# Two of eight feature-major turns taken from TensorE to VectorE block transposes and DMA through DRAM

## The reference

```
x = x + layernorm(attn(layernorm(x)))
x = x + layernorm(ffn(layernorm(x)))

attn(x): q = silu(x Wq1 Wq2);  v = x Wv
         a = exp(log_sigmoid(sigmoid(x Wk1 Wk2)));  k = 1 - a
         h[t] = a[t] h[t-1] + k[t] v[t]            (a scan over the tokens)
         out = q h;  out = out rsqrt(mean(out^2) + eps) norm_w;  return out Wo
ffn(x):  6 blocks: x = gelu(x W1' + b1) W2' + b2 + x      (256 -> 1024 -> 256)
         between blocks: x = layernorm(x) g + b
```

## Time and profile before

| | |
|---|---|
| median of 3 runs | 632.46 us (632.03 to 632.61) |
| profiled execution | 632.11 us |
| its span in the trace | 630.3 us |
| TensorE busy | 620.9 us, 2913 matmuls |
| VectorE / ScalarE / GpSimd busy | 462.5 / 407.1 / 251.8 us |
| TensorE transposes in `turn` (L490) | 56, 272 ns each |
| DMA | 24.10 MB, mean 38 GB/s |

### The profile page before, as it was taken

How to read it: one execution, slowest core, us unless ns; L and a number is a source line. 1 busy time by engine, 2 the same in 40 slices (tenths; PEclk the granted TensorE clock), 3 DMA queues, 4 the chain that set the end, 5 groups by cost and what they waited for, 6 DMA issues and landing times.

```text
span 630.3 us, 9041 instructions
## 1 busy us (share of the span) xinstructions
PE 620.9 (99%) x2913; PEld 518.0 (82%) x2913; DVE 462.5 (73%) x809; ACT 407.1 (65%) x680; POOL 251.8 (40%) x234
## 2 busy tenths in 40 slices
PE   8999999999999999999999999999999999999996
PEld 6878888887888888888888888888888888888886
DVE  6999766977676877677777768766776767677465
ACT  5989986967755666566565656755665665556454
POOL 5685413339225362324432253623255322304033
PEclk9999999999999999999999999999999999999999
DMA  8210000020111020011200110200112000003522
GB/s 289 69 36 0 2 2 0 4 71 34 37 39 40 4 70 6 12 31 37 72 5 2 40 39 15 60 6 7 36 37 72 5 4 5 6 11 77 113 72 68
DMA packets 51599, 24.10 MB, mean 38 GB/s; under 512 B 43104, under 2 KB 47584, under 8 KB 51552
## 3 DMA queue, kind: packets, MB, share of 16 engines
q1 hardware_dynamic: 51264, 23.26, 14.2%
q10 hardware_dynamic: 288, 0.26, 0.1%
HBM read 19.51 MB, written 4.00 MB: 37 GB/s over the span
## 4 chain that ended last, share of the span: by engine, by line
PE 88%; DVE 4%; issue 1%; ACT 1%; POOL 1%; DVEq 0%; ACTq 0%
PE BK L516 44%; PE BK L833 38%; PE BK L634 2%; PE BK L843 1%; PE BK L490 1%; DVE ST L391 1%; DVE BK L616 1%; POOL RN L713 0%; DVE XL L727 0%; PE BK L647 0%; DVE QB L619 0%; DVE OL L625 0%; DVE R L721 0%; DVE MV L394 0%; DVE QB L578 0%
## 5 line engine op out<-in xcount | busy, mean ns | idle before, releaser
L819 ACT ACTIVATE HH<-BK,B 128x512 fp32r<-128x512 f32 x192 | 132.1, 688 | 179.6 <-PE BK L516 177.5
L825 DVE TENSOR_TENSOR HL<-BK,HH 128x512 fp32r<-128x512 f32 x192 | 130.7, 683 | 98.2 <-ACT BK L822 97.5
L516 PE MATMUL BK<-XH,WL 128*128 128x512 f32 x416 | 162.6, 391 | 0.0
L516 PE MATMUL BK<-XL,WH 128*128 128x512 f32 x416 | 162.1, 390 | 0.0
L516 PE MATMUL BK<-XH,WH 128*128 128x512 f32 x416 | 162.0, 389 | 0.0
L833 PE MATMUL BK<-HH,WL 128*128 128x512 f32 x368 | 143.5, 390 | 0.6 <-DVE HL L825 0.6
L833 PE MATMUL BK<-HL,WH 128*128 128x512 f32 x368 | 143.2, 389 | 0.0
L833 PE MATMUL BK<-HH,WH 128*128 128x512 f32 x368 | 143.2, 389 | 0.0
L822 ACT ACTIVATE BK<-BK,B 128x512 f32<-128x512 f32 x192 | 125.4, 654 | 0.0
L516 PEld LDWEIGHTS BK<-XH,WH 128*128 128x128 f32 x416 | 78.1, 188 | 16.5
L516 PEld LDWEIGHTS BK<-XH,WL 128*128 128x128 f32 x416 | 78.1, 188 | 16.2 <-DVE XL L503 0.2
(11 more groups left out here) (136 smaller groups left out, 783.7 us busy)
## 6 DMA issues: line engine op xcount, KB each, us to landing
STG<-in_w SPq DMA_DIRECT2D x24, 512.0 KB, 3.7
G<-sums SPq DMA_DIRECT2D x160, 8.0 KB, 1.7
out<-R SPq DMA_DIRECT2D x16, 128.0 KB, 1.9
X<-in_x SPq DMA_DIRECT2D x3, 512.0 KB, 7.7
R<-turns SPq DMA_DIRECT2D x3, 512.0 KB, 4.2
sums<-P SPq DMA_DIRECT2D x40, 8.0 KB, 1.4
R<-in_wv SPq DMA_DIRECT2D x1, 512.0 KB, 5.8
STG<-in_wo SPq DMA_DIRECT2D x1, 512.0 KB, 6.2
```

What stands on the lines that cost most here:

```text
L516: r = e.matmul(dst, s, m, start=first and i == 0, stop=last and i == len(todo) - 1)
L819: lambda e, ev=ev, hs=hs, bias=bias: e.activation(HH[:, hs, :], bank_of[ev][:, :], ACT.Gelu, bias=bias),
L825: lambda e, ev=ev, hs=hs: e.tensor_tensor(HL[:, hs, :], bank_of[ev][:, :], HH[:, hs, :].bitcast(f32), ALU.subtract), ("hlo", n, j))
```

## The change

`to_features` is new and replaces `turn` in two places: l1 of tile 3 and l3 of tile 2. For each half k, VectorE transposes 32x32 blocks of the tile in R into a buffer, and four DMAs per half write it to DRAM; when all eight have landed, eight DMAs (four per half) read the feature-major tile back into R. From there ScalarE writes XH and VectorE XL. The keys of the two calls: l1 of tile 3 is normalized with key A - 20 instead of A - 11 and enters `to_features` with A - 16 instead of A - 7.5; l3 of tile 2 keeps Z + 13. The buffers lent are SA and TB, and MB; their first uses in `layer_norm` (n = 0) wait for the writes out. Semaphores that nobody waits on are no longer counted up.

```diff
+        FEATS = nc.dram_tensor("feats", (2, 2, 32, 2048), f32, kind="Internal").ap()
...
+        def to_features(key, name, t, place, tmp, ready, last_use, free):
+            slot_free[name, t] = last_use
+            swapped, moved_out, back = f"sw{place}", f"out{place}", f"back{place}"
+            rows = FEATS[place].rearrange("k j (b c m) -> k j (b c) m", b=4, c=4)
+            for k in range(2):
+                op("vector", key + 0.7 * k, [*ready, *free],
+                   lambda e, k=k: e.transpose(tmp[k].rearrange("p (b c i) -> p b c i", b=4, c=4),
+                                              feat(t, k).rearrange("p c (b j) -> p b c j", b=4)), (swapped, k))
+                for g in range(4):
+                    load(key + 1 + 0.7 * k + 0.1 * g, rows[k, :, :, 32 * g:32 * g + 32],
+                         tmp[k][32 * g:32 * g + 32].rearrange("j (b i) -> j b i", i=32), (moved_out, k, g), [(swapped, k)])
+            for k in range(2):
+                for b in range(4):
+                    load(key + 6 + 0.7 * k + 0.1 * b, feat(t, k)[32 * b:32 * b + 32],
+                         FEATS[place, k][:, 512 * b:512 * b + 512].rearrange("j (c m) -> j c m", c=4), (back, k, b),
+                         [(moved_out, 1, 3)])
+            for k in range(2):
+                op("scalar", key + 11 + 0.8 * k, [(back, 1, 3), ("slot" if k else "give", name, t)],
+                   lambda e, k=k: e.activation(by_chunk(XH[:, slot_of[name, t], k, :]), feat(t, k), ACT.Copy),
+                   ("xhi", name, t, k))
+                op("vector", key + 12 + 0.8 * k, [("xhi", name, t, k)],
+                   lambda e, k=k: e.tensor_tensor(by_chunk(XL[:, slot_of[name, t], k, :]), feat(t, k),
+                                                  by_chunk(XH[:, slot_of[name, t], k, :].bitcast(f32)), ALU.subtract),
+                   ("xlo", name, t, k))
...
-                norm(A - 11, "l1", t, R[:, t], x_of, 0.5, raw_done)
-                turn(A - 7.5, "l1", t, [("l1_nm", t, c) for c in range(4)], ("v", t, 3))
+                norm(A - (20 if t == NT - 1 else 11), "l1", t, R[:, t], x_of, 0.5, raw_done)
+                if t == NT - 1:
+                    to_features(A - 16, "l1", t, 0, [SA[:, :], TB[:, :]], [("l1_nm", t, c) for c in range(4)], ("v", t, 3), [])
+                else:
+                    turn(A - 7.5, "l1", t, [("l1_nm", t, c) for c in range(4)], ("v", t, 3))
...
-            turn(Z + 13, "l3", t, [("l3_nm", t, c) for c in range(4)], ("mm1", t, 7))
+            if t == 2:
+                to_features(Z + 13, "l3", t, 1, [MB[:, k, :] for k in range(2)], [("l3_nm", t, c) for c in range(4)], ("mm1", t, 7), [])
+            else:
+                turn(Z + 13, "l3", t, [("l3_nm", t, c) for c in range(4)], ("mm1", t, 7))
...
-                if done is None:
+                if done is None or done[0] not in waited:
                     continue
...
-                if done is not None:
+                if done is not None and done[0] in sems:
                     last.then_inc(sems[done[0]][0], step)
```

More of the change, by code:

```diff
@@ L657, in sandwich @@
             stats(Z + 1, "l2", t, p_of, lambda c, t=t: [("proj", t, m) for m in range(4)], 0.4)
-            norm(Z + 4.5, "l2", t, R[:, t], p_of, 0.3, [("turn", "l1", t, k) for k in range(2)])
+            norm(Z + 4.5, "l2", t, R[:, t], p_of, 0.3, [("turn", "l1", t, k) for k in range(2)] if t < NT - 1 else [("xlo", "l1", t, k) for k in range(2)])
             for c in range(4):
@@ L679, in before @@
                 return [(x[:-1], n - 1, 1) if x in ("nn1", "ctr1") else (x, n - 1) for x in names if n]
-            op("gpsimd", E + 1.5, [("y", n, 0), ("y", n, 1), *before("tr2")],
+            op("gpsimd", E + 1.5, [("y", n, 0), ("y", n, 1), *before("tr2"), *([("out0", 1, 3)] if n == 0 else [])],
                lambda e: e.tensor_tensor(by_chunk(SA[:, :]), feat(t, 0), feat(t, 1), ALU.add), ("sum1", n))
-            op("vector", E + 3.2, [("sum1", n), *before("red2")], lambda e: e.transpose(TB[:, :], SA[:, :]), ("tr1", n))
+            op("vector", E + 3.2, [("sum1", n), *before("red2"), *([("out0", 1, 3)] if n == 0 else [])], lambda e: e.transpose(TB[:, :], SA[:, :]), ("tr1", n))
             op("vector", E + 3.9, [("tr1", n)],
@@ L690, in layer_norm @@
                ("tot1", n))
-            op("vector", E + 10.2, [("tot1", n), *before("ctr1")],
+            op("vector", E + 10.2, [("tot1", n), *before("ctr1"), *([("out1", 1, 3)] if n == 0 else [])],
                lambda e: e.transpose(MB[:, 0, :].rearrange("p (b f) -> p b f", f=32),
@@ L713, in layer_norm @@
                lambda e: e.tensor_tensor(RN[:, :], VN[:, :], MH[:, :], ALU.pow), ("rsd", n))
-            op("vector", E + 25.5, [("rsd", n), *before("nn1")],
+            op("vector", E + 25.5, [("rsd", n), *before("nn1"), *([("out1", 1, 3)] if n == 0 else [])],
                lambda e: e.transpose(MB[:, 1, :].rearrange("p (b f) -> p b f", f=32),
@@ L922, in sandwich, with resolve @@
         slot_of.update(slots)
+        def resolve(w):
+            return prior[w] if w[0] in ("ring", "slot", "claim", "give") else None if w[0] == "after" else w
+        waited = set()
+        for q in order.values():
+            for o in q:
+                waited.update(w[0] for w in map(resolve, o[2]) if w is not None)
         owner = {}
@@ L936, in sandwich @@
                 place[done] = sems[s][1]
-        def resolve(w):
-            return prior[w] if w[0] in ("ring", "slot", "claim", "give") else None if w[0] == "after" else w
         def issue(eng, name):
```

## The result

The changed kernel is slower: 637.09 us median of 6 runs (635.88 to 639.53), against 632.5 us for the kernel before in the same session (6 runs). The ratio is 1.0082, with an interval of 1.0067 to 1.0097. The forecast was 630.7 us, and 637.09 lies above its range. The profiled execution of the changed kernel took 636.01 us (span 634.2), the one before 632.11 (630.3), so it is 3.9 us that the trace has to show.

A forecast was written before the change was run, and what follows sets the result against it. TensorE was taken to bound the kernel, busy 620.9 of 630.3 us; two removed turns gave -1.8 us and all other terms 0, so 632.46 - 1.8 = 630.7 us, range 628.9 to 634.2 us.

The forecast's parts named there:

- Two turns, -1.8 us: On TensorE, removing two groups of eight transposes, at 84 and 116.86 us, saves 0.89 us each, 1.8 us in all.
- better: Rival, chance 0.15: TensorE's HL and OL waits go too, as the tail leaves 145 to 151 us; 629.9 us.
- Slack of 2.7 us for tile 3's first norm: XL ready at 89.1 us, TensorE first takes XH at 91.81 us, so the DRAM route costs nothing.
- slower, by landing: Rival, chance 0.05: tile 3's first norm's transfers land at 5.4 us each way, TensorE stands 4.1 us; 634.8 us.
- The last norm of tile 2 in SP's order: New transfers delay the first feed-forward norm's `put1` 5.9 us and gathers 7.0 us; tile 2's XL has 12 us slack; no cost.
- The tail of the first feed-forward norm, "I leave it at 0": VectorE's R and XL at 145.6 to 150.3 us move 0 to 7 us; HL wait may go or grow; taken as 0.
- slower, by VectorE: Rival, chance 0.13: tile 2's swaps and blocked subtractions at 116 to 133 us delay OL or HL, +3.5 us; 634.2 us.
- "The order on every engine is planned anew ..., so each case has about 0.6 us to either side": Replanning every engine's order from the changed list was given about 0.6 us of spread around each case.
- Two SBUF operands in the subtractions: VectorE's four XL = R - XH might lose 0 to 4.2 us to GpSimd on the shared port; taken as 0.
- No gain, tile 3 paced by VectorE and ScalarE: Rival, chance 0.22: tile 3's attention is not paced by TensorE, which runs out of work at 133 to 160 us; 632.5 us.

The follow-up runs named there:

- The last kernel: Changed kernel with measured DMA times in the planner and the first feed-forward norm's tail behind the last HL at 166 us: 629.14 us, ratio 0.9948.
- its twin: Neither norm through DRAM, both turns on TensorE, the first feed-forward norm's tail behind that same last HL: 631.62 us, ratio 0.9988 to the kernel before.
- the late tail and true times: Changed kernel with the first feed-forward norm's tail ordered behind tile 3's last XL and the planner given 0.67 us issue, 3.1 us landing: 630.65 us.

## Why the prediction was wrong

- **Two turns, -1.8 us: right.** The reader sees it best where nothing else is in the way. The last kernel is 3.1 us faster, of which the old waits make 1.35, so the turns make 1.75. Against its twin it is 2.5 us, of which the twin's two waits make about 0.9 by their gaps; that leaves 1.5. The forecast of 630.7 us is the time of the changed kernel with true DMA times (630.37). That is partly luck: the old waits went there (-1.35) and one of 1.1 us came. The rival "better" had it right that both old waits would go; they do in the changed kernel, and were worth 1.35 us by starts, not 0.8.
- **Slack of 2.7 us for tile 3's first norm, "so I take nothing": wrong.** XL was to be there at 89.1 us and was at 93.2. The swap began at 76.41 instead of 75.2 us, because VectorE had statistics and QB in front of it (1.2). From the end of the first swap to the first read back were 7.7 us and not the 5.6 that the transfers of `turns` had shown (2.1): a write took 0.63 to 0.67 us to issue, not 0.48, and the last landed 2.93 us after its issue. The read back took 6.4 instead of 5.5 us (0.9). And TensorE came to XH 0.9 us sooner, because one of the two turns had gone by then: the slack had not been taken down by the gain itself. The rival "slower, by landing" had the place right, but took 5.4 us each way as its condition; 2.9 and 3.2 were enough.
- **The last norm of tile 2 in SP's order: right in kind, short in size.** `put1` was to go at 123.1 us and went at 126.33, the gathers 125.7 and 129.18. The delay of the gathers was 10.5 us and not 7.0: the first write went at 118.14 instead of 116.2 us, and from there to the first read back were 6.9 us instead of 5.6. XL of tile 2 came at 132.9 us against 129.8, and its slack of 12 us held.
- **The tail of the first feed-forward norm, "I leave it at 0": the step that failed.** The prediction had the tail moving by 0 to 7 us and a price of up to 4.7 us for meeting another operation, and then took the old wait of 0.6 us as the nearest row. The tail moved 7.9 us and met tile 3's XL: 3.4 us of standstill, and 1.6 us at the lower clock for which the prediction had no term. Tile 2's norm alone shows the same wait, and it goes when the norm's transfers go first, when the tail goes behind XL, or when the order is planned with true times. The rival "slower, by VectorE" had the right mechanism, an in-order VectorE in front of TensorE, at the wrong place: the swaps and subtractions at 116 to 133 us cost nothing.
- **"The order on every engine is planned anew ..., so each case has about 0.6 us to either side": wrong, and the deeper cause.** The changed kernel and the one with true times do the same work; two durations of the new DMAs in the planner, issue and landing, are all that differs, and 6.4 us lie between them, each set against the kernel before in its own session. The new DMAs entered the plan at 0.45 us and 2.1 us, and the order written for that had TensorE asking for XH and XL before they came. Neither loss needed a slower engine. True times are no cure by themselves, though: with the transfers put behind the norm's own, they left 2.3 us of waits (632.74 us).
- **Two SBUF operands in the subtractions, taken at 0: right.** All four took 0.68 to 0.69 us each. They fell where GpSimd was idle.
- **No gain, tile 3 paced by VectorE and ScalarE: refuted.** With the order mended, the time of the turns does come off the end.

What stays open is the scatter of the changed kernel, 635.88 to 639.53 us; only one run has a trace. Its two slowest runs, 639.20 and 639.53 us, have a mean clock of 0.991, the two fastest, 635.88 and 636.01, one of 0.995 and 0.996. As an estimate, 0.0045 of 636 us is 2.9 of the 3.4 us between them, so most of it is time lost at the lower clock. The estimate is rough, since the mean clock moves by 0.002 in runs of the kernel before too, and behind which waits the low clock came was not seen.

## What to carry to other kernels

Where the order of the engines is written beforehand, a transfer of a new shape is to be measured and put into the plan before the change is judged: here the same edit was 0.8% slower with the old DMA times, and 0.3% faster with measured ones. In the four pairs of kernels here that differ in these times alone, the measured ones gave 6.4, 1.8, 0.6 and 0.1 us. When one step is delayed in a queue, follow its chain to the last operation on the in-order engine and look what stands behind that there, rather than asking only whether its own reader has slack. And take from each slack what the change itself gains in front of it.

## What the runs showed of the hardware

- Behind a standstill of 3.2 us (3.0 in tile 2's norm alone) TensorE's steps took 0.43 us instead of 0.227 for about 3 us, the 1.2 GHz level: the granted clock was 0.50 from 162 to 164 us in both kernels. The wait of 1.35 us at 169 us had no such steps behind it: 0.23 us from the second on, at a granted clock of 1.00.
- A wait of TensorE costs 0.2 to 0.3 us more than the table of waits shows: 0.59 us cost 0.85, 0.87 cost 1.13, 1.35 cost 1.62. Of it 0.16 us is the way the table counts, and about 0.1 the first step behind the wait, 0.33 or 0.34 us instead of 0.227.
- A DMA of 128-byte runs from SBUF to DRAM held SP's queue for 0.63 us at the median (up to 0.67), one back 0.43; landing took 1.9 to 3.2 us in the changed kernel, and up to 3.9 in other runs of the same transfers.
- VectorE's 128x512 passes with two SBUF operands, 0.75 us at the median, took 1.1 to 1.8 us beside GpSimd's passes at 153.9 to 159.0 us; the transpose between them, with one such operand, took its ordinary 0.70. With the late tail and true times the first two passes fell where GpSimd was idle and took 0.70 us each, and the next two, beside it, 1.5. The section "Who interferes with whom" of the Trainium skill's page SBUF — State Buffer says of a port that the two share that the loser waits for the other's whole instruction. The trace agrees with the rule here, and it is what stretched the tail.
